# Own buffers for gathered expert rows and z rows, and the slot buffer's zero-fill in thirds

## What is computed

```python
x = x + tanh(g_xattn) * attention(layernorm(x), ctx, wq, wk, wv, wo)
xf = layernorm(x)
probs = softmax(xf @ gate_w.T);  top_p, top_i = top_k(probs, 2)
h   = silu(xf @ fc1[e].T) * (xf @ fc2[e].T)            # per expert e, F = 176
y   = sum over the two chosen e of top_p * (h @ proj[e].T)
s   = silu(xf @ sfc1.T) * (xf @ sfc2.T) @ sproj.T      # shared, F = 704
out = x + tanh(g_ffn) * (y + sigmoid(xf @ sgate.T) * s)
```

## Time and profile before

| | us |
|---|---|
| runs: median of 3 (lowest, highest) | 385.8 (383.8, 404.2) |
| profiled execution, from its first to its last instruction | 384.3 |
| TensorE busy | 302.6 |
| VectorE busy | 206.0 |
| ScalarE busy | 151.7 |
| POOL busy | 101.5 |

### The profile page before, as it was taken

The page is one execution under the profiler, slowest core; times in us unless marked ns, Lnnn a source line. Parts: engine busy times, 40 slices in busy tenths (PEclk is TensorE's granted clock), DMA queues, the critical chain, the costliest instruction groups (busy, mean ns, idle before and its releaser), DMA issues.

```text
span 384.3 us, 5444 instructions
## 1 busy us (share of the span) xinstructions
PE 302.6 (79%) x1808; PEld 264.9 (69%) x1808; DVE 206.0 (54%) x526; ACT 151.7 (39%) x365; POOL 101.5 (26%) x104
## 2 busy tenths in 40 slices
PE   0785699579579765696998579999999999997730
PEld 0665579458558734584886469999999978886620
DVE  2644944864765557474653535555555423374563
ACT  1543445336336412414442425655555532231200
POOL 1301212142142012047877100000000034035770
PEclk9998889999999965897899759999999999999655
DMA  8695126016114022017775443443444242037565
GB/s 263 211 383 183 56 78 200 0 61 229 43 57 159 10 109 107 1 36 251 229 245 171 138 146 101 126 124 125 125 123 128 80 137 84 0 96 248 165 191 176
DMA packets 32395, 51.85 MB, mean 135 GB/s; under 512 B 3696, under 2 KB 25072, under 8 KB 32368
## 3 DMA queue, kind: packets, MB, share of 16 engines
q1 hardware_dynamic: 28864, 42.97, 34.3%
q0 software_dynamic: 3072, 8.39, 6.9%
q10 hardware_dynamic: 432, 0.14, 0.1%
HBM read 28.68 MB, written 20.71 MB: 129 GB/s over the span
## 4 chain that ended last, share of the span: by engine, by line
PE 56%; DVE 15%; DMA 10%; issue 10%; ACT 5%; another core or an unknown queue 2%; POOL 1%; SPq 0%; DVEq 0%; ACTq 0%; POOLq 0%
PE bank L345 42%; PE bank L495 8%; DMA work<-x_dram 5%; DVE ew_lo L746 3%; PE bank L536 2%; PE bank L564 2%; DMA weight_stage<-wa_dram 2%; ACT ew_hi L587 2%; DVE ln_stats L793 2%; DVE work L789 2%; DMA xn_all<-z_d 1%; DVE xn_all L978 1%; DVE work L989 1%; DVE work L761 1%
## 5 line engine op out<-in xcount | busy, mean ns | idle before, releaser
L345 PE MATMUL bank<-ew_hi 128*128 128x256 f32 (+1 forms) x164 | 54.9, 335 | 25.6 <-ACT ew_hi L587 14.1
L1108 POOL DMA_INDIRECT xn_all<-ys_d,slot_of_pair x32 | 31.0, 969 | 130.8 <-DMA ys_d<-work 99.7
L345 PE MATMUL bank<-ew_hi,ew_lo 128*128 128x256 f32 (+1 forms) x164 | 52.1, 318 | 7.2 <-DVE ew_lo L746 7.2
L345 PE MATMUL bank<-ew_lo,ew_hi 128*128 128x256 f32 (+1 forms) x164 | 52.0, 317 | 5.0 <-DVE ew_lo L746 4.8
L345 PE MATMUL bank<-ew_hi,xt_hi 128*128 (+1 forms) x156 | 54.4, 349 | 0.6 <-DVE xt_lo L746 0.6
L345 PEld LDWEIGHTS bank<-ew_hi 128*128 128x128 f32 x164 | 32.3, 197 | 32.6 <-issue 16.0
L746 DVE TENSOR_TENSOR xt_lo<-bank,xt_hi 128x256 fp32r<-128x256 f32 (+2 forms) x86 | 38.0, 447 | 23.3 <-ACT xt_hi L587 23.3
L345 PE MATMUL bank<-ew_lo,xt_hi 128*128 (+1 forms) x156 | 47.9, 307 | 0.0
L345 PE MATMUL bank<-ew_hi,xt_lo 128*128 (+1 forms) x156 | 47.5, 305 | 0.0
L587 ACT ACTIVATE ew_hi<-bank 128x512 fp32r<-128x512 f32 (+1 forms) x57 | 29.5, 537 | 41.6 <-PE bank L345 23.3
L495 PE MATMUL bank<-sw_hi,sh_hi 128*128 128x256 f32 (+1 forms) x96 | 31.4, 327 | 17.3 <-ACT sh_hi L587 12.2
(11 more groups left out here) (103 smaller groups left out, 602.0 us busy)
## 6 DMA issues: line engine op xcount, KB each, us to landing
xs_d<-sh_hi SPq DMA_DIRECT2D x1, 4992.0 KB, 17.8
work<-xs_d SPq DMA_DIRECT2D x39, 128.0 KB, 2.2
ys_d<-work SPq DMA_DIRECT2D x39, 128.0 KB, 1.7
weight_stage<-ew_dram SPq DMA_DIRECT2D x10, 486.5 KB
work<-x_dram SPq DMA_DIRECT2D x8, 512.0 KB, 4.5
weight_stage<-sw_dram SPq DMA_DIRECT2D x4, 544.0 KB, 4.0
work<-ctx_t_dram SPq DMA_DIRECT2D x4, 512.0 KB, 7.2
x_d<-work SPq DMA_DIRECT2D x4, 512.0 KB, 2.8
```

The lines of the kernel that those rows point to most:

```text
L345: last = nc.tensor.matmul(dst, a, b, start=(n == 0), stop=(n == len(pairs) - 1))
L1108: nc.gpsimd.indirect_dma_start(out=dst[:, t % 4, :], out_offset=None, in_=ys_d, in_offset=bass.IndirectOffsetOnAxis(ap=POS[:, i, t:t + 1], ...
```

## The change

Three parts.

1. The zero-fill of `xs_d` is cut into three (13 tiles of the 39 each), issued by SP at the end of the iterations c = 0, 1 and 2, behind the load of the next quarter of the shared weights. What read the fill's semaphore now waits for three times the count.
2. `G1` and `G2` get room for all 16 tiles, in the high half of the expert weights, which are used up when the last expert projection is done. The gathers wait for that projection (and, as before, for the last expert stores), and no more for combinations. Every tile has its own semaphore.
3. z is kept in `XN`, all 16 tiles. Before the expert loop SP loads `x2_d` of chunks 2 and 3 and `z_d` of chunks 0 and 1 there, 512 KB each. The sums of s = 2 and 3 are added in place there, with no store to `z_d` and no reload; for tiles 12 to 15 the combination comes first and the sum last. Combinations 0 to 3 go behind blocks 4 and 5 of s = 2, and each block of s = 3 has two behind it. The out stores of tiles 12 to 15 wait for the sums.

```diff
@@ sync
-                    sp.dma_start(xs_d.rearrange("(n p) d -> p n d", p=P),
-                                 SH[0][:, 0:1, 0:D].bitcast(F32).broadcast_to([P, SLOT_TILES, D])).then_inc(d_zero, 16)
...
                     sp.dma_start(STF, sw[:, (c + 1) * SW_PIECE:(c + 2) * SW_PIECE]).then_inc(d_sw, 16)
+
+                    t0, t1 = c * SLOT_TILES // LAST, (c + 1) * SLOT_TILES // LAST
+                    sp.dma_start(xs_z[:, t0:t1, :],
+                                 SH[0][:, 0:1, 0:D].bitcast(F32).broadcast_to([P, t1 - t0, D])).then_inc(d_zero, 16)
...
             store_sums(1)
-            load_residual(2)
+            for c in range(2, N_CH):
+                sp.dma_start(XN[:, c * TPC:(c + 1) * TPC, :], x2_d[c]).then_inc(d_zl[c], 16)
+            sp.wait_ge(d_z, 32)
+            for c in range(2):
+                sp.dma_start(XN[:, c * TPC:(c + 1) * TPC, :], zs_d[c]).then_inc(d_zl[c], 16)
...
-            load_z(0, 4)
-            store_sums(2)
-            load_residual(3)
-            for t in range(0, 12, 4):
-                store_out(t, 4)
-                sp.wait_ge(d_out, 16 * (t + 4))
-                if t + 8 <= 12:
-                    load_z(t + 4, 4)
-            store_sums(3)
-            sp.wait_ge(d_z, 16 * N_CH)
-            load_z(12, 4)
-            store_out(12, 4)
+            for t in range(N_T - TPC):
+                sp.wait_ge(v_c2, t + 1)
+                sp.dma_start(out_t[t], XN[:, t, :]).then_inc(d_out, 16)
+            for t in range(TPC):
+                sp.wait_ge(v_z, LAST * TPC + t + 1)
+                sp.dma_start(out_t[N_T - TPC + t], XN[:, N_T - TPC + t, :]).then_inc(d_out, 16)
@@ vector, combine(t) and s_sums(s)
-                dve.wait_ge(d_zl[i], n)
-                dve.wait_ge(d_g[i], n * 2)
+                dve.wait_ge(d_zl[t // TPC], 16)
+                dve.wait_ge(d_g[t], 16 * TOP)
+                if TOP * TPC <= t < LAST * TPC:
+                    dve.wait_ge(v_z, t + 1)
...
+                    z = SX2[:, t, :] if s < 2 else XN[:, T, :]
+                    if s == LAST:
+                        dve.wait_ge(v_c2, T + 1)
@@ gpsimd
-            pool.wait_ge(d_sc, 16 * TOP * N_T)
+            pool.wait_ge(e_pj, SLOT_TILES)
...
-                if t >= 4:
-                    pool.wait_ge(v_c2, t - 3)
```

More of the change, by code:

```diff
@@ L189, in build @@
         d_ey = [sem(f"d_ey{i}") for i in range(2)]
-        d_g, d_zl = ([sem(f"d_{n}{i}") for i in range(4)] for n in ("gather", "zload"))
+        d_g = [sem(f"d_gather{t}") for t in range(N_T)]
+        d_zl = [sem(f"d_zload{s}") for s in range(N_CH)]
         zeroed, tanh_g, rw_hi, rw_lo = map(sem, ("zeroed", "tanh_g", "rw_hi", "rw_lo"))
@@ L1045, in _ @@
                     s_sums(2)
[L1046 to L1047 removed]
+                    combine(4)
+                    combine(5)
+                if j == 1:
+                    combine(6)
+                    combine(7)
+                if j == 2:
+                    combine(8)
+                    combine(9)
+                if j == 3:
+                    combine(10)
+                    combine(11)
+                if j == 4:
+                    combine(12)
+                    combine(13)
+                if j == 5:
+                    combine(14)
+                    combine(15)
             s_sums(3)
[L1049 to L1050 removed]
         @block.gpsimd
```

42 lines of the change are left out of this document (20 added, 22 removed).

## The result

The changed kernel takes **413.14 us** as a median of four runs (417.34, 417.04, 409.25, 407.42); the kernel before, on the same chip, 384.78 (379.1 to 404.16). The ratio is 1.0705, with an interval of 1.0406 to 1.1005: slower by 7%, where I forecast 375.0 and gave "slower by over 2%" a chance of 0.03.

The account below looks back on a forecast made before the run. TensorE, busy 79% of the span, was taken to bound the kernel by its waits in chunk 0 and the tail. Terms −4.1 + 7.8 + 3.4 + 1.0 − 18.9 = −10.8: span 373.5, median 375.0 us, range 368 to 382.

Parts of the forecast that it names:

- the tail's term: Behind the expert loop: waits for z rows and gathers go, so the end moves from 384.3 to 365.4, −18.9 us.
- rival A: Tail, block (3,3): ScalarE's late release, hidden before, is uncovered if gather and store traffic causes it; +3.9, 378.9 us; chance 0.26.
- Eight gathers ran from 313.25 without such an event: Tail: argument against rival A, that the first eight gathers passed without a late release of ScalarE.
- rival C: Tail: POOL's 32 gathers in a row set the end if over 1.43 us each; 384 to 400 us; chance 0.05.
- Chunk 0, −4.1: Zero-fill leaves chunk 0: VectorE's 2.4 wait for x and 1.7 of TensorE's lower clock go, −4.1 us.
- the 1.7 of clock: Chunk 0: TensorE's lower clock after idling was taken to cost 1.7 us, regained once chunk 0 runs like chunks 1 and 2.
- The thirds, +7.8 and +3.4: Chunks 1 and 2: thirds ahead of x loads add waits of 4.1 and 3.7 us, plus 1.7 of clock twice.
- The four loads before the expert loop, +1.0: Before the expert loop: three more 512 KB loads make expert tile 4 land 2.3 later; 1.2 slack leaves +1.0 us.

Follow-up runs that it names:

- e2: Changed kernel with the zero-fill in one piece in chunk 0, gathers still an unbroken train of 32: 403.4 us, 1.011 of the kernel before.
- e1: Changed kernel with one wait put back, so that at most 8 gathers are under way: 397.7 us, 0.981 of the kernel before.
- e4: Changed kernel with the gathers paced by VectorE's finished shared blocks of the tail, thirds kept: 390.6 us, 0.979 of the kernel before.
- e9: e4 with the thirds of the zero-fill moved behind the loads of x and ctx for the next chunk: 372.1 us, 0.966 of the kernel before.
- e5: Changed kernel with the zero-fill in one piece and the paced gathers of e4: 374.7 us, 0.969 of the kernel before.
- e11: Changed kernel with one fill and a small POOL operation behind every 8 gathers, no pacing: 370.9 us, 0.968 of the kernel before.
- e14: Changed kernel with one fill; behind every 8 gathers POOL waits until they have landed: 370.4 us, one run (kernel before 385.5).
- e15: Changed kernel with one fill and a small POOL operation behind the 16th and 32nd gather only: 371.7 us, one run (kernel before 385.5).
- e17: e2 again, word for word, on another chip as a control: 367.1 us, 0.951 of the kernel before.
- e18: e11 again, on the same chip as e17: 374.2 us, 0.978 of the kernel before.
- e16: e13 with the small POOL operation behind every 8 of the 32 scatters too: 373.4 us, 0.974 of the kernel before.
- e13: Changed kernel with thirds behind x and ctx loads, z loads behind the expert loop, POOL operation per 8 gathers: 367.5 us, 0.957 of the kernel before.
- e8: Changed kernel, thirds kept, with a small POOL operation behind each pair of gathers: 385.5 us, one run (kernel before 386.1).
- e6: Changed kernel with the 32 gathers replaced by plain copies from fixed rows, issued by POOL: 379.8 us, one run (kernel before 386.1).
- e7: Changed kernel with the 32 gathers replaced by plain copies from fixed rows, issued by SP: 385.8 us, one run (kernel before 386.1).

## Why the prediction was wrong

*The step that failed is the tail's term, by the size of rival A.* The tail was forecast at −18.9 and came out at +15.6 (86.6 against 71.05). I had seen the very row: at 353.14 ScalarE stands 5.67 us, released by no engine, 4.4 after its block should have ended. I called it a late release, and named the traffic of gathers as what might do it. Then I priced it as a fixed 5.67 of which +3.9 stays. But this change takes away what bounded it, the batches of 8. On the chip of the result the wait lasts until 5 us behind the end of the train, in e2 as well: 4.36 + 31.65 = 36.0 us, and e2, e1 and e4 have 30.5, 19.1 and 7.9 for a train of 32, for batches of 8 that in part ran together, and for the paced gathers. "Eight gathers ran from 313.25 without such an event" was not quite true, since the activation of block (2,2), at 321.91, comes 1.46 after the last matmul of its block instead of 0.42; and it proved nothing for 32: beside the first nine of the changed kernel's train stands a wait of 4.36 us, beside the other 23 one of 31.65. Two more waits of the kind, 2.98 and 5.72 us under the scatters, stood in the same profile, and I didn't use them.

And I looked for the danger of an unthrottled train on POOL's side alone (rival C, the spacing of the gathers), following the Trainium skill, "SBUF — State Buffer", "Who interferes with whom". POOL was never slowed: 0.95 us per gather, less than the 0.97 of before. That section also says that "PE and ACT never wait on anyone", and that a transfer never contends with a compute engine. It speaks of the ports of SBUF, and whether the stall arises there no run shows. Taken as a promise that nothing holds these engines up beside a train of transfers, it doesn't agree with ScalarE's 31.65 us and TensorE's matmuls 0.7 to 2.8 us apart; chip D's windows do agree.

*Chunk 0, −4.1.* Mis-sized. The wait of 2.4 went, but the period shrank by 1.5 only, to 33.31, with a clock of 0.90. The error was in what I compared with: the clock of 1.00 and the 30.76 us that I took for an undisturbed chunk stand in the profile of before alone. In the stretches 65 to 98 and 98 to 131 us that profile has 1.00 twice, and the nineteen others have 0.79 to 0.95, also where VectorE waits for nothing (e9: 0.90 and 0.95). So I charged the 1.7 of clock against a level that no other profile shows. The versions without a fill in front of any x load reach their first scatter 2.4 earlier than those with one fill.

*The thirds, +7.8 and +3.4.* The mechanism and the size of the waits were right: x loads of 9.62 us behind thirds, waits of 4.16 twice. Against the 30.76 of before the period grows by 7.0, where I had charged 5.8. Net with chunk 0 I had +7.1; the means of the first scatter give 179.2 − 170.6 = +8.6. The 12.45 between the two profiled executions is partly the spread of the fill in one piece, 167.3 to 173.9. That the sum of this part is a loss I had on paper before the run; the gain of the tail was to cover it.

*The four loads before the expert loop, +1.0.* As forecast between the two profiles (101.70 against 100.66), though it is less than the spread of this stretch. Larger was what neither kernel had: with these loads behind the loop instead, the stretch is some 3 to 5 us shorter.

*The tail, −18.9.* On quiet chips the tail is 53.9 to 55.8 us (e5, e9, e11, e14, e15, e17, e18), where I had walked 52.2, against 71.05 before: −15 to −17. The walk was short by 2 to 4 us, and the claim that no gather is waited for was right. On the chip of the result it is 86.6, and less the 31.5 that are extra 55.1, like the quiet ones.

*The sum.* With the measured terms of a quiet chip (+8.6, +1.0, −16) the result is −6, some 380 us: inside the range of 368 to 382, 5 above the 375.0. That is an estimate, near the upper end of the range. With the stall the kernel took 413.1, 38 above the forecast. A forecast of this change needed two cases with a chance each, stall and no stall, and the row for the first stood in the trace.

## What to carry to other kernels

A wait whose releaser the profile can't name is not a fixed cost: before removing a throttle, ask what happens if it lasts as long as the thing beside it, and give that case a chance of its own. A transfer cut in pieces is hidden only if each piece stands behind, not ahead of, the load that is waited for; in a queue taken in order the place decides, not the size (first scatter 11 us earlier with the thirds behind the x loads than with them ahead). And a cure is shown only with its untreated control on the same chip: the "cures" from e5 to e16 ran on chips B and C, with no unbroken train of gathers beside them. What beats the kernel before, on quiet chips, is the tail of this change without its thirds (e17, 0.951, but 1.011 as e2 on chip A) or with them behind x and the z loads late (e13, 0.957). Pacing the gathers helped where the chip had the stall (e4 against e2 on chip A: 390.6 against 403.4), and batches or pacing cost the tail next to nothing elsewhere (53.1 to 55.8 against the 55.0 of e17; an operation behind every pair, e8, 59.2); whether they cost nothing as a whole, e18's 7.2 us leave open.

## What the runs showed of the hardware

On chip A, and on that of the result (whether it is the same one, the records don't say), ScalarE is released late beside a long train of POOL's indirect gathers. From some 13 to 16 us after the train's start until 5 us after its end it stands (waits of 30.5 and 31.65 us), though TensorE's chain that it needs is done: 30.2 and 32.0 us lie between the chain's last matmul and the activation, and 0.43 in the runs without the stall. TensorE's next block can be slow as well, twelve matmuls over 16.8 us in the changed kernel, six over 4.5 in e2, and then it waits for ScalarE. POOL, SP and the DMA engines go on as before (0.95 us per gather, DMA share 0.33). On chip D the same program shows nothing of it. In the stall the matmuls start 0.7 us apart or at multiples of about 0.7, without a semaphore wait; what holds the sequencer and what holds the release isn't shown, nor whether the two are one thing. Whether indirect addresses are needed for it, or POOL at all, is open: the runs with plain copies (e6, e7) were on a quiet chip. What sets chip A apart is open too.

Two executions of the same code also differ by several us before the tail (first scatter 167.3 to 173.9 with the same fill), which is more than most of the terms that I summed. TensorE's clock over a chunk differs too, 0.79 to 1.00 from 98 to 131 us with the same fill.
